# Earlier loads of the second pair's attention outputs, and conditioning rows loaded from ScalarE's queue, in a fused attention and expert kernel

## The chip, the core and the metric

The kernel is one program on one core of a Trainium2 chip. The metric is the device time of one launch in microseconds (us), the median of several runs.

## The reference, cut to what matters

```python
# x: (8, 256, 1024) f32; one slot of 32 adapters and one of 8 conditioning weights for each batch
c = x @ W.T + b + 2 * (x @ A[slot].T) @ Bm[slot].T       # adapted input of the attention
q, k, v = c @ w_q, c @ w_k, c @ w_v                      # 32 heads of 32, 8 key/value heads
x = x + softmax(q k^T / sqrt(32)) v @ w_o
z = x @ weight[slot2].T                                  # (1024 x 1024) weight of the batch: "conditioning"
gates = softmax over the best 2 of 4 of (z @ router_w.T)
x = x + 4 * sum_e gates_e * ((z @ A_e.T) @ B_e.T)        # 4 experts of rank 16
```

## The kernel before, in words

The kernel is written engine by engine: for each engine a function issues its instructions in a fixed order, and semaphores tie the engines together. There are three stages. The first folds W into the q, k and v weights. The second, `attend_stage`, works through four pairs of batches; a pair has 16 steps, one for each of 8 heads' groups and 2 batches, 64 steps in all (`N = 64`, `LAST = 48` is the first step of the last pair). The third, `finish_stage`, multiplies with w_o and runs the conditioning and the experts.

**An attention step** on TensorE is: two score tiles, a slice of projection work for later groups (`WORK`), the outputs of three steps ago, a small transpose of the row maxima, transposed scores of two steps ago, two more score tiles, and a second slice of work. VectorE takes the row maxima of the four score tiles (L770) and, between the first two and the last two, evacuates projections (`late`, `soon`). A projection is split into a high and a low part: ScalarE copies the high part (L646), VectorE subtracts it (L739) for the low part. The projection buffer psP has two banks, so a projection starts only when the one two places before it in `SEQ` has been evacuated by both engines (`free` in `tensor`). In the first step VectorE evacuates q1 between the first two and the last two maxima.

**The next pair's x** comes in eight tiles k. `X_HI` says in which step and half ScalarE copies the high part of tile k (L489), `X_LO` and `X_LO_POOL` say when VectorE or GpSimd makes the low part (L493). TensorE needs tile 3 in the first half of step 12 and tile 4 in step 13, in its products with v's weight (L876 to L880).

**Work ahead.** During the last pair's steps (s = n - 48, up to s = 18) hooks of `finish_stage` run on each engine (`ahead_sync`, `ahead_scalar`, `ahead_vector`, `ahead_tensor`). w_o is loaded and split. For batches 0 and 1 attention outputs are multiplied with w_o one batch at a time, in 8 tiles (`one_tile(n, m)`, psW, L1239; a half tile is 4 of the 8 k); from pair 1 on two batches at a time (`pair_tile`). `residual` (L1230) adds a tile to x and frees its bank of psW.

**The conditioning** never forms z. For each batch the 68 rows of router and expert weights A are multiplied by the batch's conditioning weight, read as 8 rows r of blocks of 128 x 1024 (512 KB each), so there are 64 rows r = 8n + k. For a row: a load into one of 4 buffers (`RAW = 4`, L1187), ScalarE's high copy into one of 2 buffers (`cond_row_hi`, L1265), VectorE's low part (`cond_row_lo`, L1269), and 6 matmuls into psG (`cond_row`, L1284). After 8 rows ScalarE copies psG (`copy_g`, L1362), TensorE turns it in 8 small transposes (`turn_g`, L1569), ScalarE copies these (`turn_copies`, L1367), and `middle` (L1580) multiplies x by them. Then VectorE computes the gates and `y_tile` applies the experts' B, which lies in `fb_stack`, made from `fb_raw`.

**The queues.** SyncE's queue (SP in the profile, DMA queue q1) carries every load and store but the rows. For a batch n it carries four loads of reciprocal softmax denominators, spread over partitions (`rden_land`, 256 KB each), and one of 1 MB of attention values (`o_land`); `normalise` multiplies the two. GpSimd's queue (DMA queue q0) carries the rows: 0 to 3 in step s = 13, 4 and 5 in s = 16, and the others in `gpsimd`, each as soon as row r - 4 is used.

**Order of the third stage around the change.** `first` and `second` exist for each engine. On TensorE `first` is row 5, the second half of tile 7 of batch 0, row 6, row 7, the second half of tile 0 of batch 1, `turn_g(0)`, the first half of tile 1, `middle(0)`. Row 4 and the first half of tile 0 of batch 1 are the last work ahead (s = 18). `second` goes on with row 8, the second half of tile 1, row 9, tile 2, row 10, and so on. On SyncE the stage starts, once the last step's outputs are copied, with the load of the experts' B, the last pair's denominators, batch 2's values and reciprocals, batch 3's, then x of the second pair (`x_odd`).

## Time and profile before

| | |
|---|---|
| median of 3 runs | 1010.52 us (1009.11 to 1010.71) |
| the profiled execution's own time | 1010.05 us |
| its span in the profile | 1008.4 us |
| busy: TensorE, VectorE, ScalarE, GpSimd | 987.5, 625.9, 453.6, 247.2 us |
| moved by DMA | 117.33 MB, mean 116 GB/s |

The span is what the trace covers; the own time is 1.65 us more. PE is TensorE's matmuls, PEld its weight loads, DVE VectorE, ACT ScalarE, POOL GpSimd, SP SyncE. A number in square brackets behind an instruction of a timeline is how long its engine was idle before it, and what ended that. Times of instructions are from the span's start.

### The profile page before, as it was taken

The page shows a single profiled execution, that of the slowest core. Times are in us where ns is not written, and L with a number is a line of the kernel's source. Part 1 is how long each engine was busy: PE and PEld are TensorE (multiplying, and loading weights), DVE is VectorE, ACT ScalarE, POOL GpSimd, SP SyncE. Part 2 cuts the span into 40 slices and gives each one's busy share as a digit, 9 for nine tenths or more (in the row PEclk, how much of TensorE's full clock was granted, in tenths as well). Part 3 has the DMA queues.
Part 4 walks back from the last instruction along what each step waited for, and adds up shares of the span by engine and source line. Part 5 has one row for each costly group of instructions (what it writes and reads, how often), then busy time and mean ns, then how long its engine had stood idle before and what let it go on. Part 6 is the DMA issues. An engine that isn't in the chain of part 4 may idle for free.

```text
span 1008.4 us, 16074 instructions
## 1 busy us (share of the span) xinstructions
PE 987.5 (98%) x6228; PEld 769.9 (76%) x6228; DVE 625.9 (62%) x1028; ACT 453.6 (45%) x806; POOL 247.2 (25%) x234
## 2 busy tenths in 40 slices
PE   9999999999999999999999999999999999999996
PEld 6878788777687776877777777786787778778775
DVE  6671822686946778467786688766664654654443
ACT  6121322365744657456665566747441432332221
POOL 1000001033422434223343247645110110110001
PEclk9999999999999999999999999999999999999999
DMA  7030411111411124111142424264999579463432
GB/s 274 0 105 1 136 48 56 43 44 39 128 36 44 50 59 123 44 44 49 44 114 79 110 74 138 86 170 185 276 298 251 165 248 243 143 223 108 164 125 84
DMA packets 72395, 117.33 MB, mean 116 GB/s; under 512 B 7698, under 2 KB 55186, under 8 KB 70816
## 3 DMA queue, kind: packets, MB, share of 16 engines
q1 hardware_dynamic: 62592, 81.70, 28.5%
q0 software_dynamic: 9728, 34.61, 10.0%
q8 instruction: 50, 0.82, 0.4%
q14 instruction: 25, 0.20, 0.1%
HBM read 86.38 MB, written 18.89 MB: 104 GB/s over the span
## 4 chain that ended last, share of the span: by engine, by line
PE 92%; DVE 4%; ACT 1%; POOL 1%; issue 1%; DMA 1%; POOLq 0%; ACTq 0%
PE psP L854 21%; PE psW L1239 17%; PE psF L292 12%; PE psG L1284 8%; PE psO L950 6%; PE psS L926 6%; PE psT L937 5%; PE psX L1580 3%; PE psO L954 3%; DVE nmax L770 2%; PE psF L303 2%; PE psP L876 2%; DVE q_stack L739 1%; PE psP L878 1%; PE psM L961 1%; PE psP L880 1%
## 5 line engine op out<-in xcount | busy, mean ns | idle before, releaser
L630 POOL TENSOR_TENSOR p_sum<-probs 128x512 f32<-128x512 f32 x128 | 168.5, 1317 | 331.7 <-ACT probs L681 331.7
L854 PE MATMUL psP<-x_hl,wq 128*128 128x512 f32 x960 | 237.2, 391 | 0.2 <-DVE v_sb L760 0.2
L770 DVE TENSOR_REDUCE nmax<-psS 128x2 f32<-128x512 f32 x256 | 164.5, 684 | 96.2 <-PE psS L926 91.8
L854 PEld LDWEIGHTS psP<-x_hl,wq 128*128 128x128 f32 x960 | 173.4, 188 | 31.2 <-DVE v_sb L760 0.4
L681 ACT ACTIVATE probs<-psT 128x512 f32<-128x512 f32 x256 | 139.0, 595 | 74.2 <-PE psT L937 73.4
L1239 PE MATMUL psW<-o_split,wq 128*128 128x512 f32 (+1 forms) x600 | 137.5, 383 | 0.0
L1239 PEld LDWEIGHTS psW<-o_split,wq 128*128 128x128 f32 x600 | 108.8, 188 | 21.4
L1269 DVE TENSOR_TENSOR cond_lo<-cond_raw,cond_hi 128x1024 fp32r<-128x1024 f32 x64 | 78.3, 1240 | 54.8 <-ACT cond_hi L1265 54.3
L1265 ACT ACTIVATE cond_hi<-cond_raw 128x1024 fp32r<-128x1024 f32 x64 | 66.5, 1057 | 82.9 <-PE psG L1284 70.2
L739 DVE TENSOR_TENSOR q_stack<-psP,q_stack 32x512 fp32r<-32x512 f32 x128 | 87.8, 686 | 10.2 <-ACT q_stack L646 8.3
L926 PEld LDWEIGHTS psS<-k_stack,q_stack 96*128 96x128 f32 x512 | 79.0, 189 | 16.5 <-DVE q_stack L739 2.1
L1187 POOL DMA_DIRECT2D cond_raw<-in_cond x64 | 33.9, 530 | 232.8 <-PE psG L1284 232.8
L937 PE MATMUL psT<-q_stack,k_stack 98*128 98x512 f32 x256 | 86.8, 418 | 0.0
L926 PE MATMUL psS<-k_stack,q_stack 96*128 96x256 f32 x512 | 84.6, 285 | 1.9 <-DVE nmax L770 1.3
L646 ACT ACTIVATE q_stack<-psP 32x512 fp32r<-32x512 f32 x128 | 75.1, 587 | 17.3 <-PE psP L861 15.8
L292 PE MATMUL psF<-q_hi,w_hi 128*128 128x512 f32 x184 | 71.8, 390 | 0.0
L292 PE MATMUL psF<-q_lo,w_hi 128*128 128x512 f32 x184 | 71.6, 389 | 0.0
L292 PE MATMUL psF<-q_hi,w_lo 128*128 128x512 f32 x184 | 71.6, 389 | 0.0
L950 PE MATMUL psO<-probs,v_sb 128*32 128x256 f32 x1024 | 68.5, 385 | 0.0
L699 ACT ACTIVATE nmax_rows<-psM 16x128 f32<-16x128 f32 x64 | 17.0, 266 | 105.1 <-PE psM L961 104.7
L950 PEld LDWEIGHTS psO<-probs,v_sb 128*32 128x32 f32 x1024 | 26.7, 109 | 30.1 <-issue 16.3
L1239 PE MATMUL psW<-wq 128*128 128x256 f32 x384 | 49.4, 283 | 0.0
(155 smaller groups left out, 1378.4 us busy)
## 6 DMA issues: line engine op xcount, KB each, us to landing
cond_raw<-in_cond POOLq DMA_DIRECT2D x64, 512.0 KB, 4.8
x_raw<-in_xT SPq DMA_DIRECT2D x32, 256.0 KB, 3.2
o_scratch<-o_sb SPq DMA_DIRECT2D x64, 128.0 KB
q_stack<-q_stack SPq DMA_DIRECT2D x31, 256.0 KB, 2.9
q_raw<-in_Wqkv SPq DMA_DIRECT2D x24, 256.0 KB, 3.9
o_pair<-rden_scratch SPq DMA_DIRECT2D x24, 256.0 KB, 9.0
o_pair<-o_scratch SPq DMA_DIRECT2D x6, 1024.0 KB, 13.9
w_raw<-in_W SPq DMA_DIRECT2D x8, 512.0 KB, 7.8
```

The costliest lines, as they stand in the source:

```text
L292: mm = pe.matmul(psF[:, bank(j, m)], w[:, k, m * P:(m + 1) * P], q[:, k], start=(k == 0 and i == 0), stop=(k == KT - 1 and i == 2))
L630: pool.tensor_tensor(p_sum[:, heads], probs[:, 0, heads], probs[:, 1, heads], ALU.add).then_inc(sum_done, 1)
L681: nc.scalar.activation(probs[:, i % 2, (i // 2) * 512:(i // 2 + 1) * 512], psT[:, i % 2], ACT.Exp, scale=ATT_SCALE).then_inc(exp_done, 1)
L739: ins = dve.tensor_tensor(to(h), both(psP[32 * h:32 * h + 32, bank(p, u)]), f(hi(h)), ALU.subtract)
L770: dve.tensor_reduce(nmax[:, n % 2, 2 * hp:2 * hp + 2, qt], psS[:, i % 2].rearrange("p (h k) -> p h k", h=2), AX.X, ALU.max, negate=True).t ...
L854: mm = pe.matmul(out, wq[:, i, w, k * P:(k + 1) * P], x[:, k, part], start=(k == 0 and n_ == 0), stop=False)
L926: mm = pe.matmul(psS[:, i % 2, j * T:(j + 1) * T], q_stack[0:96, slot, c, 2 * hp + j, qt * P:(qt + 1) * P], k_stack[0:96, c, g], start=Tru ...
L937: pe.matmul(psT[:, kt], k_stack[0:98, c, g, kt * P:(kt + 1) * P], q_stack[0:98, slot, c, 2 * hp:2 * hp + 2].rearrange("p h t -> p (h t)"), ...
L950: pe.matmul(psO[HD * h:HD * h + HD, 0], v_sb[p % 2][:, c, kt, g], probs[:, kt, h * T:(h + 1) * T], start=(kt == 0), stop=(kt == KK - 1))
L1239: mm = pe.matmul(out, wq[:, k, w, m * P:(m + 1) * P], o(part, k), start=(k == 0 and j == 0), stop=(k == KT - 1 and j == 2))
L1269: dve.tensor_tensor(cond_lo[r % RAW][:], cond_raw[r % RAW][:], f(cond_hi[:, r % SPLIT]), ALU.subtract).then_inc(cond_lo_done, 1)
L1284: mm = pe.matmul(psG[0:EC, half], a[:, k], w[:, half * 512:(half + 1) * 512], start=(k == 0 and i == 0), stop=(k == KT - 1 and i == 2))
```

## The change: what it does

- In `attend_stage` the high part of x tile 4 moves on ScalarE from the first to the second half of step 11, and the low part of tile 3 moves on VectorE from the second to the first half of step 11. In the first step VectorE evacuates q1 behind all four maxima.
- The experts' B is loaded in step s = 14, the values of batches 2 and 3 in s = 17 into a place of their own (`o_second`, the blocks from which tile 7 of batch 0 is read, so that tile is brought forward: its halves run in s = 16 and s = 17), and their reciprocals at the start of s = 18. SyncE waits for both batches before it loads `x_odd`; the last pair's reciprocals are computed and stored later.
- Rows 6 to 63 are loaded by ScalarE's queue: in `cond_row_hi(r)`, after its waits and before its copy, ScalarE reads the slot number and issues the load of row r + 2. GpSimd loads rows 0 to 5 as before.
- TensorE's order in `first` and `second` moves on by half a tile, and `turn_copies(0)` goes ahead of the high copy of row 9.

```diff
-X_HI = {(10, 1): range(4), (11, 0): [4], (12, 0): [5, 6], (12, 1): [7]}
-X_LO = {(11, 0): [0, 1], (11, 1): [3], (12, 1): [5, 6], (13, 0): [7]}
+X_HI = {(10, 1): range(4), (11, 1): [4], (12, 0): [5, 6], (12, 1): [7]}
+X_LO = {(11, 0): [0, 1, 3], (12, 1): [5, 6], (13, 0): [7]}
...
-            for unit_ in late(n - 1) if n else [(0, "q1")]:
+            for unit_ in late(n - 1):
                 evacuate(*unit_)
...
                 split_maxima(n)
+            if n == 0:
+                evacuate(0, "q1")
...
+    FIRST_ROWS = 6
...
+    o_second = at("o_second", [P, KT, 2, T], F32, O_EVEN + KT * 2 * T * 4)
...
-    cond_landed = [sem(f"cond_landed{i}") for i in range(RAW)]
+    cond_landed, cond_behind = ([sem(f"{name}{i}") for i in range(RAW)] for name in ("cond_landed", "cond_behind"))
...
     def o_land(n):
-        return o_raw[:, 1 - n, 1] if n < 2 else o_pair[n // 2 % 2][:, 1, :, n % 2]
+        if n < 2:
+            return o_raw[:, 1 - n, 1]
+        return o_second[:, :, n % 2] if n < 4 else o_pair[n // 2 % 2][:, 1, :, n % 2]
...
-    def load_o(sp, n):
-        if n >= 4:
-            sp.wait_ge(wo_done, tile(n // 2 - 1, 0))
+    def load_rden(sp, n):
         sp.wait_ge(before.rden_stored, 16 * (n // 2 + 1))
         for h in range(HG):
             sp.dma_start(rden_land(n)[HD * h:HD * h + HD], rden_scratch[n, h:h + 1].to_broadcast([HD, G, T])
                          ).then_inc(o_landed[n % 2], 16)
+
+    def load_values(sp, n):
         sp.dma_start(o_land(n), oT[n]).then_inc(o_landed[n % 2], 16)
+
+    def load_o(sp, n):
+        if n >= 4:
+            sp.wait_ge(wo_done, tile(n // 2 - 1, 0))
+        if n == 4:
+            sp.wait_ge(o_lo_done, 4)
+        load_rden(sp, n)
+        load_values(sp, n)
...
+            if s == 18:
+
+                sp.wait_ge(before.st_done, 4 * N)
+                for n_ in (2, 3):
+                    load_rden(sp, n_)
             return
...
+        if s == 14:
+
+            sp.wait_ge(before.st_done, 4 * (LAST + 12))
+            for half in range(2):
+                sp.dma_start(fb_raw[ER * half:ER * (half + 1)], ffn_B).then_inc(fb_landed, 16)
+        if s == 17:
+            sp.wait_ge(wo_done, KT)
+            for n_ in (2, 3):
+                load_values(sp, n_)
...
-        for half in range(2):
-            sp.dma_start(fb_raw[ER * half:ER * (half + 1)], ffn_B).then_inc(fb_landed, 16)
         before.load_den(sp, PAIRS - 1)
-        load_o(sp, 2)
-        before.store_rden(sp, PAIRS - 1)
-        load_o(sp, 3)
+
+        for c in range(2):
+            sp.wait_ge(o_landed[c], 16 * (HG + 1) * 2)
         for m in range(KT):
+            if m == 4:
+
+                before.store_rden(sp, PAIRS - 1)
             if m == 6:
...
-    def load_cond(pool, n, ks):
-        slot = pool.value_load(idx_sb[0:1, n:n + 1], min_val=0, max_val=7)
+    def landed(r):
+
+        if r < FIRST_ROWS:
+            return cond_landed[r % RAW], r // RAW + 1
+        return cond_behind[r % RAW], (r - FIRST_ROWS) // RAW + 1
+
+    def load_cond(engine, n, ks):
+        slot = engine.value_load(idx_sb[0:1, n:n + 1], min_val=0, max_val=7)
         for k in ks:
-            if KT * n + k >= RAW:
-                pool.wait_ge(cond_used, KT * n + k - RAW + 1)
-            pool.dma_start(cond_raw[k % RAW][:], cond2[bass.ds(slot, 1), k].rearrange("s p d -> (s p) d")
-                           ).then_inc(cond_landed[k % RAW], 16)
+            r = KT * n + k
+            if r >= RAW:
+                engine.wait_ge(cond_used, r - RAW + 1)
+            engine.dma_start(cond_raw[r % RAW][:], cond2[bass.ds(slot, 1), k].rearrange("s p d -> (s p) d")
+                           ).then_inc(landed(r)[0], 16)

     def gpsimd(pool):
-        for n in range(B):
-            load_cond(pool, n, range(6, KT) if n == 0 else range(KT))
...
     def cond_row_hi(act, r):
-        act.wait_ge(cond_landed[r % RAW], 16 * (r // RAW + 1))
+        act.wait_ge(landed(r)[0], 16 * landed(r)[1])
         if r >= SPLIT:
             act.wait_ge(cond_used, r - SPLIT + 1)
+        if FIRST_ROWS - 2 <= r < KT * B - 2:
+
+            load_cond(act, (r + 2) // KT, [(r + 2) % KT])
         nc.scalar.activation(cond_hi[:, r % SPLIT], cond_raw[r % RAW][:], ACT.Copy).then_inc(cond_hi_done, 1)
...
+        if part == 1 and s == 17:
+            residual(dve, KT - 1)
...
-        if (n - LAST, part) == (17, 0):
-            one_tile(pe, 0, KT - 1, range(4))
+        if (n - LAST, part) in ((16, 0), (17, 0)):
+            one_tile(pe, 0, KT - 1, range(4) if n - LAST == 16 else range(4, KT))
...
             cond_row_hi(act, KT)
+            turn_copies(0)
             cond_row_hi(act, KT + 1)
-            turn_copies(0)
...
             cond_row_lo(dve, 6)
             dve.memset(beats[:], 0.0).then_inc(chain, 1)
+            residual(dve, KT)
             cond_row_lo(dve, 7)
-            residual(dve, KT - 1)
-            before.invert(dve, PAIRS - 1)
...
         def second():
-            residual(dve, KT)
+            residual(dve, KT + 1)
             gates(0)
             for m in range(KT):
-                if m:
+                if m > 1:
                     residual(dve, KT + m)
...
+                if m == 1:
+                    before.invert(dve, PAIRS - 1)
...
             cond_row(pe, 5)
-            one_tile(pe, 0, KT - 1, range(4, KT))
+            one_tile(pe, 1, 0, range(4, KT))
             cond_row(pe, 6)
             cond_row(pe, 7)
-            one_tile(pe, 1, 0, range(4, KT))
+            one_tile(pe, 1, 1, range(4))
             turn_g(0)
-            one_tile(pe, 1, 1, range(4))
+            one_tile(pe, 1, 1, range(4, KT))
             middle(0)
...
             for m in range(1, KT - 1):
-                one_tile(pe, 1, m, range(4, KT) if m == 1 else range(KT))
+                if m > 1:
+                    one_tile(pe, 1, m)
                 cond_row(pe, KT + m)
```

## Rows read from the trace of the kernel before

**Rows 1.** The page: its span, and the busy time of each engine.
```profile
span 1008.4 us, 16074 instructions
...
PE 987.5 (98%) x6228; PEld 769.9 (76%) x6228; DVE 625.9 (62%) x1028; ACT 453.6 (45%) x806; POOL 247.2 (25%) x234
```

**Rows 2.** Busy time by window, one row; last are clock, DMA share, GB/s.
```profile
705.00:725.00 20.00, 18.60 (x140) 14.23 (x140) 10.82 (x14) 8.80 (x11) 4.16 (x7) 1.00 0.92 270
```

**Rows 3.** Waits of TensorE, whole span: total us, times, longest us.
```profile
PE psP L876 <- DVE q_stack L739: 2.6, 3, 0.9
PE psP L876 <- DVE x_hl L493: 1.8, 3, 0.6
...
PE psG L1284 <- DVE nmax L770: 0.3, 1, 0.3
```

**Rows 4.** TensorE in order of time, the first attention steps.
```profile
192.99 1.01 PE L926 MATMUL psS<-k_stack,q_stack 96*128 96x256 f32 x4 [0.85 <-DVE nmax L770]
...
197.30 1.66 PE L854 MATMUL psP<-x_hl,wq 128*128 128x512 f32 x6 [0.20 <-DVE v_sb L760]
```

**Rows 5.** VectorE in order of time, the first attention steps.
```profile
189.34 2.79 DVE L739 TENSOR_TENSOR q_stack<-psP,q_stack 32x512 fp32r<-32x512 f32 x4
...
196.56 0.69 DVE L760 TENSOR_TENSOR v_sb<-v_sb,psP 128x512 f32<-128x512 f32 x1 [1.50 <-PE psP L889]
```

**Rows 6.** VectorE in order of time, steps 11 and 12 of pair 0.
```profile
266.96 1.29 DVE L770 TENSOR_REDUCE nmax<-psS 128x2 f32<-128x512 f32 x2 [0.59 <-PE psS L926]
...
269.10 0.68 DVE L493 TENSOR_TENSOR x_hl<-x_raw,x_hl 128x512 fp32r<-128x512 f32 x1
```

**Rows 7.** ScalarE in order of time, around the end of attention.
```profile
707.28 1.05 ACT L1265 ACTIVATE cond_hi<-cond_raw 128x1024 fp32r<-128x1024 f32 x1
711.02 1.06 ACT L1265 ACTIVATE cond_hi<-cond_raw 128x1024 fp32r<-128x1024 f32 x1 [2.70 <-DMA cond_raw<-in_cond]
713.15 1.06 ACT L1265 ACTIVATE cond_hi<-cond_raw 128x1024 fp32r<-128x1024 f32 x1 [1.07 <-DMA cond_raw<-in_cond]
```

**Rows 8.** TensorE in order of time, the same stretch.
```profile
713.40 0.68 PE L1284 MATMUL psG<-cond_hi,ra_hi 128*68 128x512 f32 x2 [0.73 <-DVE cond_lo L1269]
...
715.52 0.68 PE L1284 MATMUL psG<-cond_hi,ra_hi 128*68 128x512 f32 x2 [0.51 <-DVE cond_lo L1269]
...
718.41 0.66 PE L1569 MATMUL psX<-id_sb,g_sb 68*128 68x68 f32 x8
...
720.71 3.79 PE L1580 MATMUL psX<-g_t,x_even 128*128 128x68 f32 x32 [0.15 <-ACT g_t L1367]
```

**Rows 9.** SyncE's queue in order of time, the same stretch.
```profile
703.68 0.52 SPq L575 DMA_DIRECT2D den_scratch<-o_sb  x1
```

**Rows 10.** VectorE in order of time, row 7's low part.
```profile
714.24 1.23 DVE L1269 TENSOR_TENSOR cond_lo<-cond_raw,cond_hi 128x1024 fp32r<-128x1024 f32 x1 [0.86 <-ACT cond_hi L1265]
```

**Rows 11.** Chain of waits: start us, us, what; the second part of stage three.
```profile
725.89 1.43 PE psW L1239 x12
...
728.74 2.86 PE psW L1239 x24
731.60 1.37 PE psG L1284 x6
```

**Rows 12.** Row loads issued at 680 to 681, 715 to 718, 750 to 751.5 us.
```profile
cond_raw<-in_cond POOLq DMA_DIRECT2D x1, 512.0 KB, 10.5
cond_raw<-in_cond POOLq DMA_DIRECT2D x2, 512.0 KB, 8.5
cond_raw<-in_cond POOLq DMA_DIRECT2D x1, 512.0 KB, 3.8
```

**Rows 13.** DMA queues from 716 to 720 us: packets, MB, share of 16 engines.
```profile
q1 hardware_dynamic: 968, 0.89, 109.2%
q0 software_dynamic: 20, 0.05, 3.8%
```

**Rows 14.** DMA queue of SyncE from 725 to 728 us, the same columns.
```profile
q1 hardware_dynamic: 1058, 0.99, 109.5%
```

More of the change, by code:

```diff
@@ L439, in attend_stage @@
     st.exp_done, st.pv_done, st.o_copied, st.o_stored = exp_done, pv_done, o_copied, o_stored
+    st.st_done = st_done
     st.rden_stored, st.x_used = rden_stored, x_used
```

## The prediction, made before the changed kernel was run

> **What bounds the kernel now.** I read the page first: TensorE is busy for 987.5 us of a span of 1008.4 [rows 1], so time can only come out of places where TensorE stands still or starts late. The waits of TensorE, taken over the whole span, name the few places [rows 3]: three waits of about 0.9 us for VectorE's low part of a projection, three of 0.6 us for an x tile, and one of 0.3 us for the row maxima. The windows then show that the densest gap of the third stage lies between 705 and 725 us: TensorE is busy for 18.6 of 20 us there, and the DMA engines' share is 0.92 [rows 2]. So there are two separate bounds in what the change touches: VectorE's order inside attention steps, and the landing of rows 6 and 7 after the last step. The sum is made against the profiled execution's own time, 1010.05 us (span 1008.4 plus 1.65); it lies 0.47 us, 0.05%, under the median of 1010.52. About 0.2%, 2.0 us, is what a measurement of this kernel can tell from no change.
>
> **Part A, the first step's evacuation of q1.** TensorE waits 0.85 us for the third maximum [rows 4], because VectorE evacuates q1 first: 2.79 us from 189.34 [rows 5]. With the maxima first this wait goes. But VectorE stays the bound: the same four subtractions still have to be done before the product r0 may take q1's bank, and before the next step's maxima. Laid out by hand, VectorE does the maxima at 190.4, the split by 192.2, q1 until 195.1, the next two maxima until 196.4, then the addition of r0 that stood at 196.56 [rows 5], on which TensorE waits at 197.30 [rows 4]. The addition starts 0.15 us earlier, so of 0.85 us only **0.15 us** is kept. Bounds: 0 and 0.85; I take 0.15, as the addition's own row sets it.
>
> **Part B, the x splits.** In steps 11 and 12 VectorE is idle 0.59 us before the maxima at 266.96, and then does the low part of tile 3 at 269.10 in 0.68 us, for which TensorE waits 0.60 us, three times, once for each next pair [rows 3, 6]. Moved to the first half of step 11 the subtraction falls into the idle time, and VectorE's later work, the evacuation of q7 that ends TensorE's other wait of 0.86 us [rows 3], moves up with it. That second wait stays as long as it was, since both sides shift. Late next is the second half of that step's maxima, by the 0.1 us by which the subtraction is longer than the idle time, less its overlap: I take 0.57 us a pair, **1.7 us** for three. What it costs: ScalarE's high copy of tile 4 now stands behind the four copies of q7, and GpSimd's low part of tile 4 behind it; TensorE needs that tile only in step 13, a whole step later. If that cover were gone, each pair would lose what it wins. Bounds: 0 and 1.8 us.
>
> **Part C, the half tile brought forward.** In s = 16 TensorE now has half a tile (1.43 us [rows 11]) ahead of row 0, so its wait for the last maxima, 0.3 us [rows 3] and a slower first matmul of about 0.15 us, is filled: **0.45 us**. When it comes to row 6, it has done one more half tile than before. Before, it was free at 712.67 (713.40 less 0.73 idle) [rows 8]; now it comes at 712.67 + 1.43 - 0.45 = 713.65 us.
>
> **Part D, the loads moved forward, and what they collide with.** Before, row 6's high copy waited for its load until 711.02 and row 7's until 713.15 [rows 7]; TensorE stood idle 0.73 us and 0.51 us for them and 0.15 us before `middle(0)` [rows 8]. 1.39 us could be had here. But SyncE now issues, right behind the stores that stood at 703.68 [rows 9] and by my count at 705.0 us after part C's shift, 2 MB of values, and from about 706 eight loads of reciprocals, 2 MB, which drain slowly. ScalarE issues row 6's load in `cond_row_hi(4)`, about 705.5, and row 7's in `cond_row_hi(5)`, which waits for the copy of the last outputs and stood at 707.28 [rows 7]; with TensorE later by a half tile less the 0.45 us (1.43 - 0.45) it becomes 708.3 us. So row 7 is asked for later than before, and behind more bytes.
>
> How long does it take? The extremes are 3.8 us with nothing else in flight and 10.5 us for the last of four rows behind outputs of batch 1; two rows that met reciprocals took 8.5 us [rows 12]. Why 8.5: from 716 to 720 us SyncE's queue had 109% of the engines and the rows' queue 3.8%, although two rows were asked for; the reciprocals moved 0.89 MB in these 4 us [rows 13]. So the two queues take turns in large pieces, and a row waits out a piece of about 1 MB. Values are faster than reciprocals: 0.99 MB in 3 us [rows 14]. A piece of 1 MB costs 3.0 us in values against 4.5 us in reciprocals, so a row behind values should take 8.5 - 1.5 = 7.0 us, and I take 6.7 us, since the piece has begun when the row arrives. Row 6 lands at 705.5 + 6.7 = 712.2, row 7 at 708.3 + 6.7 = 715.0. The Trainium skill, "DMA: Bandwidth & Descriptors" (Queues, rings and completion order), states that each DMA engine goes round between the queues that have work, one packet at a time, with at most 64 descriptors in a packet; the trace agrees in kind, as q0 gets 3.8% in one stretch and most of another. No run here shows ScalarE's queue at all.
>
> From landing to TensorE a row needs a high copy of 1.06 us [rows 7] and a low part of 1.23 us [rows 10], with 0.1 us between them 2.4 us in all. Row 6 is ready at 714.6 (a wait of 0.95 us), done at 716.0; row 7 is ready at 717.4, done at 718.8. Then half a tile, `turn_g` (0.66 us with its tail, 0.5 until the next start [rows 8]), half a tile: 722.15. `middle(0)` wants `turn_copies(0)`, which now stands behind row 8's high copy only; but row 8 is asked for when row 6 has landed, 712.2, and behind reciprocals takes 8.5 us [rows 12]: 720.7, high copy until 721.8, copies until 722.45. `middle(0)` 3.79 us [rows 8], rows 8 and 9 1.37 us each, tile 2 2.86 us: row 10 starts at 731.85, against 731.60 before [rows 11]. Parts C and D together are **0.3 us worse**, where without any wait they would be 1.84 us better.
>
> **Part E, parts that I cost at nothing.** The load of the experts' B in s = 14 falls beside rows 1 to 3, of which the next is wanted some 7 us later. SyncE's order: the stores of the last step's outputs and the last denominators now stand behind eight loads; VectorE inverts them only after row 11's low part, near 732 us, when I expect them landed at 731; each us beyond is a us of VectorE, with a tile and a row of 2.86 + 1.37 us [rows 11] as cover. `x_odd` is wanted only by the second pair, after 760 us. ScalarE's 58 issues: before row 5 the issue lies beside the copy of the last outputs; if the sequencer takes it serially, row 5 is late by up to 0.5 us, since this chain was just in time. Elsewhere a row comes every 4.23 us, and ScalarE's copy takes 1.06. In the pairs tiles are twice as wide, so the time between rows is longer still. Bounds of this part: -0.3 (a load from ScalarE's queue could land a little sooner) and +1.0.
>
> **Sum:** 1010.05 - 0.15 - 1.7 + 0.3 = **1008.5 us**.
>
> **The rivals.**
> 1. *The rows come in time* (0.33). ScalarE's queue may get its turn before the values' piece starts, or both rows may go in one turn; for it: two queues share by turns, and row 6 is asked for only half a us behind the values. Then only A, B and C stand, and the waits before rows 6, 7 and `middle(0)` go: 1010.05 - 0.15 - 1.7 - 1.84 = 1006.4 us. It decides when row 7 lands by 712.6 to 713. The Trainium skill, "SBUF — State Buffer" (SBUF: two separate sides), speaks for it in its own way: a load issued from GpSimd can starve while VectorE holds the port pair that the two share, and one issued from ScalarE can't. No row shows such starving here: GpSimd's loads land in 3.8 us when nothing else is in flight [rows 12].
> 2. *Slower: rows 6 and 7 queue behind all of SyncE's loads* (0.17). If ScalarE's requests wait for what SyncE has already asked for, each takes the 10.5 us of [rows 12]: row 6 at 716.0, row 7 at 718.8, and every us of row 7 is a us of the span: 1008.5 + 3.8 = 1012.3 us. It decides from a landing of 10.3 us on, where the time passes 1012.1. For it: 2 MB of values and 2 MB of reciprocals are a larger burst than any row met before. Against it: rows asked for later than SyncE's loads were served within 8.5 us, though SyncE's queue never ran empty [rows 12, 13].
> 3. *The x split only moves the wait* (0.10). If TensorE waits instead for tile 4, or VectorE's maxima come later by what was won, B gives nothing: 1008.5 + 1.7 = 1010.2 us.
>
> The forecast itself has 0.40. **The numbers:** 1008.5 us. The range goes from 1005.9, rival 1 with 0.5 us of luck in A and E, to 1012.2, just short of rival 2. Faster by over 2.0 us needs row 7 to land by 714.5: rival 1 and a little of the forecast, 0.39. Slower by as much is rival 2 and a tail of part E, 0.19. Within: 0.42.
>
> **What would show it.** In the profile after: TensorE's waits for x_hl gone and the one for q_stack still three times 0.9; no wait of psG for nmax; the high copies of rows 6 and 7 at about 712.2 and 715.0, less what A and B took off (1.85 us), each preceded by a wait for a load; two waits of TensorE for cond_lo of about 1 and 1.4 us; from row 12 on none. The forecast is wrong if those waits are gone or above 3 us, if TensorE waits in the pairs for rows, if ScalarE's copies show idle time put down to its own issues, or if VectorE stands before its inversion.

## The result, and the profile after

| | before | after |
|---|---|---|
| median of 20 runs each | 1010.02 us | 1012.32 us |
| lowest, highest | 1008.35, 1012.13 | 1010.78, 1015.91 |
| the profiled execution's own time (span) | 1010.05 (1008.4) | 1013.26 (1011.5) |
| ratio, 95% interval | | 1.0029 (1.0021 to 1.0037) |

The changed kernel is slower by 0.29%, about 2.9 us (2.3 us between the two medians). Forecast were 1008.5 us and a range up to 1012.2, so the sign is wrong and the median lies just outside the range. Two executions in the experiments, at a mean granted clock of 0.76 and 0.85 and 8 to 20% longer than the rest, are left out of all counts, medians and ratios.

The page answers to [rows 1]:

```profile
span 1011.5 us, 16228 instructions
...
PE 990.2 (98%) x6228; PEld 770.8 (76%) x6228; DVE 625.2 (62%) x1028; ACT 457.3 (45%) x806; POOL 216.1 (21%) x176
```

and the same window as in [rows 2], with the same columns:

```profile
705.00:725.00 20.00, 16.49 (x108) 11.23 (x106) 6.38 (x7) 8.00 (x9) 1.28 (x1) 0.91 1.03 304
```

TensorE works 2.1 us less in the same 20 us (18.60 before), its granted clock is 0.91 instead of 1.00, and the DMA engines are fuller (1.03 for 0.92). Busy time over the whole span grew by 2.7 us though the number of matmuls is the same: part of the loss is not idle time but slower matmuls.

The waits of TensorE over the whole span, against [rows 3]:

```profile
PE psG L1323 <- DVE cond_lo L1308: 3.5, 2, 3.0
PE psP L879 <- DVE q_stack L740: 2.6, 3, 0.9
...
PE psX L1622 <- ACT g_t L1408: 1.3, 2, 0.7
```

The waits for x_hl and for the last maxima are gone, those for q_stack are what they were. New are 3.5 us for two low parts of rows and 1.3 us for g_t. TensorE in order of time, in place of [rows 8]:

```profile
717.06 0.73 PE L1323 MATMUL psG<-cond_hi,ra_hi 128*68 128x512 f32 x2 [3.05 <-DVE cond_lo L1308]
717.59 1.05 PE L1323 MATMUL psG<-cond_lo,ra_hi 128*68 128x512 f32 x2
...
725.73 0.44 PE L1622 MATMUL psX<-g_t,x_even 128*128 128x68 f32 x2 [0.71 <-ACT g_t L1408]
...
735.17 0.69 PE L1323 MATMUL psG<-cond_hi,ra_hi 128*68 128x512 f32 x2
```

TensorE waits 3.05 us for row 6 and then runs rows 6 and 7 at 1.05 us for two matmuls instead of 0.62 to 0.68. Row 10 starts at 735.17, where it started at 731.60 before [rows 11]. At the transpose of step 60 both kernels had stood level (662.21 and 662.17), so those 3.5 us are lost behind the steps.

Why row 6 is late shows on ScalarE, in place of [rows 7]; ACTq is its queue's issues:

```profile
706.11 0.39 ACTq L1225 DMA_DIRECT2D cond_raw<-in_cond  x1
...
708.21 0.35 ACTq L1225 DMA_DIRECT2D cond_raw<-in_cond  x1
...
714.29 0.35 ACTq L1225 DMA_DIRECT2D cond_raw<-in_cond  x1
714.69 1.06 ACT L1304 ACTIVATE cond_hi<-cond_raw 128x1024 fp32r<-128x1024 f32 x1 [5.02 <-issue]
...
723.65 0.35 ACTq L1225 DMA_DIRECT2D cond_raw<-in_cond  x1
724.04 1.06 ACT L1304 ACTIVATE cond_hi<-cond_raw 128x1024 fp32r<-128x1024 f32 x1 [1.36 <-issue]
```

By the trace's DMA view the row asked for at 706.11 landed after 7.3 us (713.4), the one of 708.21 after 6.8 us (715.0), the one of 714.29 after 8.6 us (722.9). Row 6's high copy starts at 714.69, 1.3 us behind its landing, since ScalarE first reads the slot number and issues row 8. Row 8's copy is 1.1 us behind its landing in the same way.

Where the time of the two profiled executions went, by anchors on TensorE:

| stretch | before | after | difference |
|---|---|---|---|
| start to step 60 | 662.17 | 662.21 | 0.04 |
| step 60 to row 10 | 69.43 | 72.96 | +3.53 |
| row 10 to `middle(1)` | 23.37 | 24.08 | +0.7 |
| `middle(1)` to the end | 253.4 | 252.2 | -1.2 |

The first line holds 2.1 us of gain (parts A and B) and a start that came 2.1 us later in this one execution: TensorE's first score tile started at 189.71 us, at 187.58 before, and at 186.9 to 187.7 in the traces of the experiments quoted below. The last line is not in the pairs. From `middle(1)` to GpSimd's last addition both kernels take 246.6 us; the 1.2 us lie behind it, in the last stores and the end of the program. Every trace with ScalarE's rows has this gain and none with GpSimd's, so the queue of the change gives back about 1.1 us at the end of whatever it costs ahead of it. No run shows what the gain comes from.

### The profile page after: what moved, and what is told of

It reads as the page before. It is cut to its first block, busy times and chain, and to the rows that moved or that the text cites. A ratio compares the mean times of both kernels' runs of the same rounds, so it can differ in the third digit from the quotient of the medians.

```text
span 1011.5 us, 16228 instructions
## 1 busy us (share of the span) xinstructions
PE 990.2 (98%) x6228; PEld 770.8 (76%) x6228; DVE 625.2 (62%) x1028; ACT 457.3 (45%) x806; POOL 216.1 (21%) x176
## 4 chain that ended last, share of the span: by engine, by line
PE 88%; DVE 7%; DMA 2%; issue 1%; ACT 1%; ACTq 0%; POOL 0%; POOLq 0%; SPq 0%
PE psP L857 20%; PE psW L1275 17%; PE psF L292 12%; PE psG L1323 8%; PE psO L953 5%; PE psT L940 5%; PE psS L929 5%; DVE nmax L771 3%; PE psX L1622 3%; PE psO L957 2%; DVE q_stack L740 2%; PE psF L303 2%; DMA cond_raw<-in_cond 2%; PE psP L879 2%; PE psP L881 1%; PE psP L883 1%
## 5 line engine op out<-in xcount | busy, mean ns | idle before, releaser
L1234 POOL TENSOR_TENSOR x_odd<-x_odd,y_sb 128x512 f32<-128x512 f32 x4 | 5.0, 1280 | 294.1 <-DVE gated L1519 294.1
```

## The experiments

After the first look I had two theories: the early loads of values and reciprocals hold rows 6 and 7 back, whoever asks for them (theory 1), and ScalarE's queue costs by itself (theory 2). Later came a wider form of theory 1: the stretch from 700 to 745 us is bound by the DMA engines, so that a load moved within it moves the wait. The rivals: that TensorE's order or a load of the experts' B was the loss. All ratios are to the kernel before, run on the same chip, with 95% intervals; n is the number of runs. A trace shows one execution, which need not lie near its kernel's median; where it lies over 2 us off, its time is given.

**Parts A and B alone.** The kernel before with

```diff
-X_HI = {(10, 1): range(4), (11, 0): [4], (12, 0): [5, 6], (12, 1): [7]}
-X_LO = {(11, 0): [0, 1], (11, 1): [3], (12, 1): [5, 6], (13, 0): [7]}
+X_HI = {(10, 1): range(4), (11, 1): [4], (12, 0): [5, 6], (12, 1): [7]}
+X_LO = {(11, 0): [0, 1, 3], (12, 1): [5, 6], (13, 0): [7]}
...
-            for unit_ in late(n - 1) if n else [(0, "q1")]:
+            for unit_ in late(n - 1):
...
+            if n == 0:
+                evacuate(0, "q1")
```

> The kernel before with the attention parts of the change alone (A and B). In the two profiles A and B together took 2.1 us out of TensorE's way between its first steps and step 64, while the start was 2.1 us later for another reason. If A and B are worth this by themselves, the time is 2.0 us under the kernel before (ratio 0.998). Rival (the split only moves the wait): no difference, within 0.3 us.

Measured: 0.9976 (0.9964 to 0.9988), n = 11, median 1007.97. By the ratio that is 2.4 us (1.4 us between the medians), and every trace with A and B is 2.1 us shorter between the first score tile and the last steps; A and B were forecast at 1.85. So the rest of the change costs 0.5% on top.

**Undoing the queue, the early loads, and both.**

```diff
+        for n in range(B):
+            load_cond(pool, n, range(6, KT) if n == 0 else range(KT))
...
-        if FIRST_ROWS - 2 <= r < KT * B - 2:
-            load_cond(act, (r + 2) // KT, [(r + 2) % KT])
```

> The changed kernel, but rows 6 to 63 are loaded by GpSimd again; SyncE's loads stay early. Theory 1 (the early 4 MB of values and reciprocals hold rows 6 and 7 back, whoever asks for them): rows 6 and 7 still land 7 to 9 us after their issue, TensorE still waits 2 to 4 us for row 6, and the time stays 1 to 2.5 us over the kernel before. Theory 2 (ScalarE's queue is the cause: the loads are asked for late and one after the other): TensorE's wait for row 6 falls under 1 us and the time is 2 to 3.5 us under the kernel before.

Measured: 1.0014 (1.0006 to 1.0023), n = 11. By the two ratios the queue costs 1.5 us of the 2.9, though the intervals just overlap. Row 6 still comes late (TensorE waits 3.31 us at 714.02), but its copy now starts at its landing, and both rows were asked for by 704.7 us. Row 6 took 7.5 us to land from GpSimd's queue, 7.3 us from ScalarE's. In that trace the clock stayed at 1.00, but it is the fastest of the 11 runs, 1008.36 us, and the only one with a mean granted clock of 0.998; the ten others have 0.992 to 0.996 and take 1.4 to 3.4 us more.

```diff
-            if s == 18:
-                sp.wait_ge(before.st_done, 4 * N)
-                for n_ in (2, 3):
-                    load_rden(sp, n_)
...
-        if s == 17:
-            sp.wait_ge(wo_done, KT)
-            for n_ in (2, 3):
-                load_values(sp, n_)
...
         before.load_den(sp, PAIRS - 1)
+        load_o(sp, 2)
+        load_o(sp, 3)
```

> The changed kernel, but values and reciprocals of batches 2 and 3 are loaded after the last step again; rows 6 to 63 stay on ScalarE's queue. Theory 1: rows 6 and 7 land 4 to 5 us after their issue, TensorE waits less than 1 us for them in all, its clock doesn't fall, and the time is 3 to 3.5 us under the kernel before (ratio 0.997). Theory 2: rows still come late, the time is 0 to 2 us over the kernel before.

Measured: 1.0003 (0.9991 to 1.0015), n = 12. So undoing the early loads, with the queue left on ScalarE, takes 2.6 us off. The run before met theory 1's forecast (1 to 2.5 us over), this one theory 2's (0 to 2 us over, where theory 1 said 0.997): neither carries the whole loss.

Both edits together:

> Both undone: rows by GpSimd, values and reciprocals loaded late; A, B, the half tile brought forward, the experts' B early and the order of the copies stay. Both theories: 3 to 3.7 us under the kernel before (A and B 2.0, C and the waits of rows 6, 7 and middle(0) 1 to 1.8). If e3 and e4 are equal, the queue that asks for the rows is worth nothing either way.

Measured: 1.0044 (1.0031 to 1.0057), n = 5. This contradicts every sum of parts: by the ratios, undoing the two suspects made the kernel no faster than the change itself, and if anything slower. In its trace (1010.10 us, the fastest of the five; their median is 1013.66) `middle(0)` starts 3.3 us earlier than in the kernel before, and `middle(1)` does not: TensorE waits 2.6 us at 744 us for x_even. I come back to it below.

**The queue alone**, on top of A and B, loads and order as before.

> The kernel before with A and B, and rows 6 to 63 loaded by ScalarE's queue; nothing of SyncE's loads or of TensorE's order is changed. e1 (A and B alone) measured 0.9976. Theory 2 (the queue costs by itself: row 7 is asked for behind ScalarE's work, row r + 2 only when row r has landed, and each issue stands in front of a copy): 1 to 3 us slower than e1, with TensorE's waits before rows 5, 6 and 7 0.5 us longer each. Rival (the queue costs only in company of the early loads): equal to e1 within 0.5 us.

Measured: 1.0029 (1.0011 to 1.0047), n = 12, against 0.9976 without it. In its trace `middle(0)` waits 1.91 us for g_t, because `turn_copies(0)` stands behind the copies of rows 8 and 9, each held up by a landing and an issue. TensorE, and the window in which the clock is lowest:

```profile
720.53 4.90 PE L1591 MATMUL psX<-g_t,x_even 128*128 128x68 f32 x32 [1.91 <-ACT g_t L1378]
```

```profile
725.00:730.00 5.00, 5.00 (x21) 3.92 (x21) 2.55 (x17) 1.04 (x2) 0.00 (x0) 0.52 1.14 231
```

The clock is at 0.52, the lower level of 1.2 GHz, from 725 to 730 us, behind waits of 0.59, 1.40 and 1.91 us within 13 us. `middle(0)` takes 4.90 us instead of 3.79 [rows 8].

**Later reciprocals, earlier values.** Two tries to place the early loads better, with GpSimd's rows.

```diff
-                for n_ in (2, 3):
-                    load_rden(sp, n_)
...
+        load_rden(sp, 2)
         before.load_den(sp, PAIRS - 1)
+        load_rden(sp, 3)
```

> The changed kernel with rows by GpSimd and only the values loaded early (s = 17); the reciprocals are asked for behind the last step's stores. If it is the values, asked for 1.5 us before rows 6 and 7, that hold these back: TensorE still waits over 2 us for row 6, as in e2 (3.31 us). If it is the reciprocals: under 1 us. I expect the first, and 0 to 1 us less than e2 in all.

Measured: 1.0001 (0.9989 to 1.0012), n = 11, against 1.0014: at best 0.13%, within the intervals. TensorE's wait for row 6 is still there, 3.45 us at 714.77. In addition, values asked for in s = 16 and tile 7 half a step earlier:

```diff
-        if s == 17:
+        if s == 16:
             sp.wait_ge(wo_done, KT)
...
-        if (n - LAST, part) in ((16, 0), (17, 0)):
+        if (n - LAST, part) in ((15, 1), (16, 0)):
```

> As e6, but tile 7 of batch 0 runs a step earlier (second half of s = 15, first half of s = 16), so that the values are loaded in s = 16, when the DMA engines have little to do. Theory 1 in its wider form (the stretch from 700 to 745 us is bound by DMA: rows 6 and 7 at its start, the values of batch 3 at its end; a load moved inside the stretch only moves the wait, one moved out of it takes it away): rows 6 and 7 land in 4 to 5.5 us, no wait of TensorE over 0.7 us before 760, and the time is 3.5 to 4.5 us under the kernel before (ratio 0.996). If it is not better than e1 (0.9976), the theory falls.

Measured: 1.0006 (0.9996 to 1.0016), n = 11: a miss. The values now meet rows 4 and 5 instead of 6 and 7. ScalarE in this kernel's trace (1012.13 us, the slowest of the 11; their median is 1009.98):

```profile
707.41 1.06 ACT L1300 ACTIVATE cond_hi<-cond_raw 128x1024 fp32r<-128x1024 f32 x1 [3.41 <-DMA cond_raw<-in_cond]
```

TensorE waits 2.10 us at 709.78, and the granted clock is 0.56 from 710 to 715. By the sign set for it (not better than A and B alone) the wider theory fell in this form: the load was not moved out of the full stretch, the stretch only began earlier, with a DMA share of 1.02 from 700 to 705 us, where it is 0.58 before. With ScalarE's rows:

> e7 with rows 6 to 63 on ScalarE's queue. If the queue costs 1.5 us wherever the rows are just in time (after against e2), e8 is 1 to 2 us slower than e7; row 5 waits 0.5 us for the issue in front of its copy, and row 7 is asked for 1.5 us later. Rival: with the bound gone the queue doesn't matter, and they are equal within 0.4 us.

Measured: 1.0045 (1.0029 to 1.0060), n = 12; the queue costs 0.4% here too.

**Is it the queue, or when it asks?** The load of row r + 2 is issued ahead of the wait for row r:

```diff
-        act.wait_ge(landed(r)[0], 16 * landed(r)[1])
         if r >= SPLIT:
             act.wait_ge(cond_used, r - SPLIT + 1)
         if FIRST_ROWS - 2 <= r < KT * B - 2:
             load_cond(act, (r + 2) // KT, [(r + 2) % KT])
+        act.wait_ge(landed(r)[0], 16 * landed(r)[1])
```

In the changed kernel:

> The changed kernel, but ScalarE issues the load of row r + 2 ahead of its wait for row r's landing instead of behind it. If ScalarE's queue costs because row r + 2 is asked for only when row r has landed, row 8 is asked for some 5 us before the 714.29 us of the changed kernel, middle(0)'s wait of 0.71 us for g_t goes, and the ratio to the kernel before falls from 1.003 to about 1.001, that of the changed kernel with GpSimd's rows. Rival: what costs is ScalarE's queue itself (0.4 us of issue ahead of each copy, and its turn among the queues); then the ratio stays at 1.003.

Measured: 1.0004 (0.9993 to 1.0014), n = 12, where the change has 1.0029. On A and B alone:

> The kernel before with parts A and B and the rows from the seventh on by ScalarE's queue, each asked for ahead of ScalarE's wait for the row in front. Without the change of place the ratio was 1.0029, with GpSimd's rows 0.9976. If the late asking was the cause, it comes back to 0.998; if ScalarE's queue itself is, it stays at 1.003.

Measured: 1.0000 (0.9985 to 1.0015), n = 12, where it had 1.0029. So asking late costs 0.25 to 0.29%; in the changed kernel the intervals are apart, on A and B alone they just overlap. ScalarE in the first of the two, the changed kernel with the load asked for first:

```profile
708.64 0.35 ACTq L1225 DMA_DIRECT2D cond_raw<-in_cond  x1
709.26 1.06 ACT L1304 ACTIVATE cond_hi<-cond_raw 128x1024 fp32r<-128x1024 f32 x1 [2.19 <-DMA cond_raw<-in_cond]
```

Row 8 is asked for at 708.64 instead of 714.29, and row 6's copy starts when the row lands (6.4 us after 702.89), with nothing between them. The wait of 0.71 us before `middle(0)` is gone, but not the one at `middle(1)` (0.53 us), and two others are left: 1.71 us for a row at 714.96 and 2.38 us for x_even at 737.15. The latter stands behind SyncE's order: VectorE waits 3.19 us for the last denominators before it inverts them, at 735.87. In the second kernel of the two VectorE stands 3.31 us for batch 3's values. The difference that is left between this and GpSimd's rows is within the intervals of the changed kernel (1.0004 and 1.0014); of A and B (1.0000 and 0.9976) the intervals barely touch, and what makes that difference is not settled.

**Filling the gaps with work.** If idle time ahead of rows 6 and 7 is what costs, half tiles in front of them would give it back. In the changed kernel with GpSimd's rows:

```diff
             one_tile(pe, 1, 0, range(4, KT))
+            one_tile(pe, 1, 1, range(4))
             cond_row(pe, 6)
+            one_tile(pe, 1, 1, range(4, KT))
             cond_row(pe, 7)
-            one_tile(pe, 1, 1, range(4))
             turn_g(0)
-            one_tile(pe, 1, 1, range(4, KT))
+            one_tile(pe, 1, 2, range(4))
             middle(0)
```

> The changed kernel with GpSimd's rows, and on TensorE the two halves of tile 1 stand ahead of rows 6 and 7 (the first half of tile 2 ahead of middle(0)), so that its idle time of 3.3 us before row 6 has 1.43 us of work and the time before row 7 as much. If the idle time, with the fall of the clock that follows it in some executions, is what the early loads cost, then the ratio falls from 1.0014 to about 0.998, and the granted clock stays 1.00 from 710 to 725 us. Rival: the stretch is bound by DMA up to the values of batch 3, and the work moved up leaves the same gap behind it (before middle(0), rows 8 to 10 or the x_even wait near 744 us); then the ratio stays at 1.001.

Measured: 1.0008 (0.9998 to 1.0019), n = 12, against 1.0014: no gain that stands out. The wait at 714.6 is still 2.45 us, the granted clock is 0.72 from 715 to 720 us, and `turn_g(0)` now waits 1.2 us for ScalarE's copy of psG. The same idea on A and B alone:

> The kernel before with parts A and B, and on TensorE the second half of tile 0 ahead of row 6 and the first half of tile 1 ahead of row 7; loads and queues as before. Its two waits for rows (1.6 and 1.0 us) are filled. If they bound the end, the ratio falls from 0.9976 by 2 us to 0.9956. Rival: VectorE's wait for the values of batch 3, which land near 741 us whatever TensorE does, takes it all: middle(0) starts 2 us earlier, middle(1) when it did (755.3 us), TensorE's wait of 1.4 us near 745 us grows to 3.4 us, and the ratio stays at 0.9976 or rises by what the clock loses.

Measured: 0.9984 (0.9973 to 0.9995), n = 12, against 0.9976: nothing gained by removing 2.6 us of waits ahead of rows 6 and 7, since `turn_g(0)` now waits 1.20 us for ScalarE's copy of psG.

**The order of TensorE's tiles (part C), the experts' B, and SyncE's order.** The fourth experiment left open which of the cheap parts costs. On top of A and B, the order alone (its edit is that of the change in TensorE's tiles of s = 16 and s = 17, in `first` and `second`, in `residual`, and in `turn_copies(0)`):

> Parts A and B (0.9976) and TensorE's order of the change (part C), all loads and queues as before. If the order is harmless, as my prediction had it (0.45 us of gain that a wait for row 6 or the values takes back), the ratio is 0.997 to 0.998. If the order is what costs, since the work that covered the landing of rows 6 and 7 now lies ahead of the last step's end and pushes their asking back, it is 1.002 or more, with TensorE's waits for cond_lo above 3 us in all.

Measured: 1.0005 (0.9991 to 1.0019), n = 11, median 1008.71. It lies between the two answers expected. By the ratios it is up by 0.29% from 0.9976, with intervals that just miss each other; the two medians differ by 0.7 us only. With the experts' B loaded in s = 14 as well:

> As e13, and the experts' B loaded in step s = 14. It takes 0.25 MB off the stretch in which the DMA engines are full, so it should be the same as e13 or up to 0.001 lower; a rise would say that the early load delays rows or w_o in the attention steps.

Measured: 1.0034 (1.0016 to 1.0052), n = 12, median 1013.78: not the small gain that was expected. With SyncE's order too, which is the fourth experiment's kernel again:

> As e14, and SyncE stores the last reciprocals only between the loads of the second pair's x, which it starts only when the values of batches 2 and 3 have landed, VectorE inverting later: this is the kernel of e4 again. If e4's five runs were right it is 1.004, and if e14 is then at 0.998 SyncE's order is the cause: the wait of TensorE for x_even near 744 us would be there in e15 and gone in e14. If it comes out near 0.999, e4's few runs misled.

Measured: 1.0034 (1.0017 to 1.0050), n = 9, in line with 1.0044: the few runs had not misled. And the load of the experts' B without the order:

> Parts A and B and the early load of the experts' B, nothing else. 0.25 MB less stand ahead of the second pair's values and rows 6 and 7: VectorE's wait for the values and TensorE's 1.4 us near 745 us shrink by about 0.8 us, so 0.997, if the load is free where it now stands; 0.998 or more if not.

Measured: 0.9975 (0.9961 to 0.9989), n = 11, median 1007.15. The load of the experts' B is free by itself. The pair that shows the order's cost best is this kernel and the one with the order on top, 0.9975 and 1.0034: 0.59%, or 6.6 us between the medians. The same step without the experts' B is smaller (0.9976 to 1.0005), and the order and that load together are worst.

The traces of this pair say why; both lie near their kernel's median (1007.44 of 1007.15, and 1013.62 of 1013.78). VectorE in order of time at the outputs of batch 3, first in the kernel before:

```profile
741.59 2.29 DVE L1202 TENSOR_TENSOR o_pair<-o_pair 128x2048 f32<-128x2048 f32 x1
```

with A and B and the experts' B:

```profile
739.29 2.28 DVE L1208 TENSOR_TENSOR o_pair<-o_pair 128x2048 f32<-128x2048 f32 x1
```

and with the order too:

```profile
744.03 2.29 DVE L1208 TENSOR_TENSOR o_pair<-o_pair 128x2048 f32<-128x2048 f32 x1 [5.82 <-DMA o_pair<-o_scratch]
```

In the kernel before the values land just in time: asked for at 724.27, they land after 16.7 us, at 741.0, 0.6 us before VectorE takes them. In the second kernel it is the same (722.16 and 16.6 us, 0.5 us before). With the order they are asked for at 722.67 and land after 21.3 us; VectorE stands in `normalise(3)` until they have landed, and the residual that frees TensorE's bank of psW stands behind it. TensorE with the order and the experts' B:

```profile
746.71 5.49 PE L1245 MATMUL psW<-wq 128*128 128x256 f32 x24 [5.04 <-DVE x_even L1236]
```

Its window in which the clock is lowest (the clock is the third number from the end):

```profile
745.00:750.00 5.00, 3.29 (x15) 3.30 (x16) 5.00 (x6) 1.91 (x1) 0.00 (x0) 0.52 0.78 271
```

With the order TensorE frees the rows' buffers earlier, so GpSimd asks for the rows earlier: at 724.52, 728.76 and 733.02 us instead of 726.73, 730.96 and 735.22. The DMA engines are at 1.0 and above until 745 us in both, so what the rows get the values lack: from 725 to 735 us the rows' queue moves 1.52 MB instead of 1.05, and SyncE's 1.29 MB instead of 1.78. A wait of 5.04 us follows, and behind it a tile at half clock that takes 5.49 us instead of 3.14.

The order without the experts' B shows the same bytes (1.56 and 1.35 MB, against 0.96 and 1.78 with A and B alone) and a wait of 3.07 us for x_even at 743.97, but its trace can't be set against that of A and B alone: the latter (1010.35 us) is a slow one among runs with a median of 1007.97, has a wait of 1.40 us in the same place, and is longer than that with the order (1008.57).

The same shows in the pair of kernels that have TensorE's order and late values and differ in the row queue alone. SyncE asks for batch 3's values and, when they have landed, for x of the second pair. With GpSimd's rows:

```profile
723.69 1.90 SPq L1119 DMA_DIRECT2D o_second<-o_scratch  x1
745.70 2.00 SPq L1130 DMA_DIRECT2D x_odd<-in_xT  x4
```

With ScalarE's rows:

```profile
722.00 0.65 SPq L1119 DMA_DIRECT2D o_second<-o_scratch  x1
738.51 2.84 SPq L1130 DMA_DIRECT2D x_odd<-in_xT  x4
```

The values need 22.0 us against 16.5 (the second trace is of 1012.11 us, its kernel's median 1010.00; its excess is a lower clock behind 755 us). ScalarE's queue asks for its rows later (724.61, 728.60 and 735.12 us against 723.44, 724.83, 729.06 and 733.32). There it is a gain (1.0003 against 1.0034), I take it because the engines are left to the transfer that is wanted; that part is not tested by itself. With the values early the queue is a loss (1.0029 against 1.0014). No version tried is clearly better than A and B alone; with the experts' B in s = 14 it has the lowest median, 1007.15 us, and the same ratio.

## Why the prediction was wrong, step by step

- **A and B: right.** Forecast 1.85 us; 2.4 us by the ratio of the runs of both alone, 2.1 us by the anchors. A gave 0.2 of these (the first score tile behind step 0 starts 14.32 us after the first of all before, 14.08 after the change), B the other 1.9. The waits for x_hl went, the one for q_stack stayed three times 0.9 us.
- **C: the term held in the changed kernel; what it does to later transfers had no step.** The wait for the maxima went. TensorE was ready for row 6 at 714.01 (717.06 less 3.05), forecast 713.65, with a wait of 0.46 us before row 5 in between. The prediction had no step for the landing of batch 3's values, although in the kernel before they landed 0.6 us ahead of their use, and part C's sum ended at row 10, three tiles before it. Where the values are loaded late, that is what the order costs (0.59% in the clearest pair). It is not what slowed the changed kernel: there the values are early, both normalisations (740.20 and 744.74) start without idle time on VectorE, and TensorE has no wait for x_even. No run takes the order alone out of the changed kernel.
- **D: the mechanism right, its size wrong by 3.3 us. This is the first step that failed.** Row 10 was forecast at 731.85 and started at 735.17. The landing time was well taken: 6.7 us forecast, 7.3 and 6.8 measured; 8.5 us for row 8, and 8.6 measured. What failed is mostly the step from landing to matmul. Row 6 was asked for 0.6 us later than forecast, landed 0.6 us slower, and its copy began 1.3 us behind the landing, where the sum had nothing: 2.5 us, so that TensorE, which itself came 0.4 us later than forecast, waited 3.05 us instead of 0.95. Row 8 inherited that and added 1.1 us of its own between landing and copy: `middle(0)` at 725.73 instead of 722.45.
- **E: "the issues cost nothing" is the step that failed there.** It priced an issue at 0.5 us, before row 5 alone (0.46 us measured), and held the others to be covered by 4.23 us a row. It missed that the issue stands behind a wait for the landing, so that reading the slot and issuing lie between landing and copy on the very rows that TensorE waits for, and that row r + 2 is asked for only when row r has landed. Putting the issue ahead of the wait gave 0.25% back in the changed kernel, 0.29% on A and B alone. Part E's other worry, VectorE before its inversion, did not show in the changed kernel (736.50, no idle time). The gain of 1.1 us at the end of the program had no term either.
- **The clock was left out.** Behind the wait of 3.05 us rows 6 and 7 took 4.40 us from 717.06 instead of 2 x 1.37 [rows 11]: 1.7 us that no term held. I had taken TensorE's work at the durations of a stretch whose granted clock was 1.00 [rows 2].
- **The rivals.** Rival 2 gave about the time that was measured (1012.3), by luck and by another mechanism: the rows did not land after 10.5 us. Rival 1's condition, row 7 landed by 712.6 to 713, was missed (715.0). Rival 3 was wrong: B gives what it was priced at. The Trainium skill, "DMA: Bandwidth & Descriptors" (Issuing engines are not separate DMA queues), says that transfers of all issuing engines run on the same 16 DMA engines and interleave, and that issuing from several of them saves only the time of issuing. The traces agree with the first half (from 725 to 735 us, with A, B and the experts' B, SyncE's queue has 73.8% and the rows' 34.1% of the engines) and add to the second that where the issue stands in its engine's order cost more than the issue itself: 1.1 to 1.3 us a row for an issue of 0.35 us.

What stays open: why A and B with ScalarE's queue asked first (1.0000) is behind GpSimd's rows (0.9976), and how the loss of each version divides between idle time and clock. The times of one kernel often fall in two groups: with the order and the experts' B three runs of 12 took 1008.7 to 1010.3 us at a mean granted clock of 0.996 to 0.998, nine took 1013.0 to 1016.9 at 0.992 to 0.995; with A, B and the queue asked first four of 12 took 1007.0 to 1007.5 at 0.998 to 0.999, as fast as A and B alone. So a part of several ratios is how often the clock fell. The mean granted clock doesn't follow the times in all versions: it is 0.9968 for A and B, 0.9933 for the queue alone on top of them and 0.9967 for the changed kernel with the loads asked for first, but 0.9936 for the changed kernel with GpSimd's rows, at 1.0014; the kernel before had 0.995 to 0.997 on the same chips.

## What to carry to other kernels

Where the DMA engines are full up to a date, moving loads, or the work that asks for them, within that stretch decides mostly which consumer is late: before pricing such a move, look for the transfers that land just in time behind the place you mend, and end the sum at the last of them. A load that an engine issues for later use belongs ahead of its wait for the present one, not between that wait and the work the wait was for. And idle time of TensorE of some 2 to 5 us is to be priced with what the slower clock behind it may cost.

## What the runs showed of the hardware

- Behind waits of 1.9 to 5.0 us in a stretch that was busy before, TensorE's granted clock fell to its lower level of 1.2 GHz for a few us: 0.76 over 715 to 720 in the changed kernel (3.05 us idle), 0.56 over 710 to 715 (2.10 us idle, values in s = 16), 0.72 over 715 to 720 (2.45 us idle, gaps filled, GpSimd's rows), 0.52 over 745 to 750 (5.04 us idle). It did not always: after 3.07 us in the kernel with the order alone, and 3.31 us in the changed kernel with GpSimd's rows, every window stayed at 1.00. Of the latter kernel this was the exception, one run of 11 by the mean granted clock (0.998, the others 0.992 to 0.996). The Trainium skill, "TensorE: Matmul & The Clock Gate" (What's actually happening), says that the clock is throttled when the engine has been idle and freed again by activity; the traces agree in kind, and no run here shows what decides between the two outcomes.
- A load issued by ScalarE takes 0.35 to 0.39 us of its queue, but put behind a wait in the changed kernel it delayed the copies of rows 6 and 8 by 1.3 and 1.1 us, the reading of the slot number included.
- 1 MB of values took 16.6 or 21.3 us to land in two kernels that differ in TensorE's order alone, and so in how early the rows were asked for on another queue (16.5 and 22.0 us in the pair that differs in the rows' queue).
- The end of the program, from the start of TensorE's last product with g_t, took 16.6 us in every trace with GpSimd's rows and 15.4 to 15.5 us in every trace with ScalarE's.
